# GpSimd's scatters in a graph kernel: a 128x112 product ahead of each, in place of one one-element operation per slot of 17

## What is computed

```python
xn = _layernorm(x)
x = x + L0_gnn(xn, src, dst)          # edge softmax: gathers x[src] for every edge, sums by dst
      + L0_mix(xn)                    # linear attention and an MLP, dense
x = x + L0_ffn(_layernorm(x))         # top-k of the nodes, MLP
xn = _layernorm(x)
x = x + L1_gnn(xn, edge_weight, W, b, src, dst) + L1_mix(xn)
x = x + L1_ffn(_layernorm(x))         # two chosen experts

def _L1_gnn_ref(x, edge_val, W, b, edge_row, edge_col):
    support = jnp.matmul(x, W)
    gathered = support[edge_col] * edge_val[:, None]
    out = jax.ops.segment_sum(gathered, edge_row, num_segments=x.shape[0])
    return out + b
```

## Time and profile before

| | us |
|---|---|
| median of three runs | 6699.03 |
| span of the profiled execution | 9414.7 |
| GpSimd busy in it | 4691.2 |
| of that, 1564 scatters (line 557) | 1532.7 |
| of that, 3128 gathers (line 1794) | 2980.2 |
| TensorE busy | 5293.0 |
| VectorE busy | 3692.5 |

### The profile page before, as it was taken

The page is one execution under the profiler, slowest core; times in us unless marked ns, Lnnn a source line. Parts: engine busy times, 40 slices in busy tenths (PEclk is TensorE's granted clock), DMA queues, the critical chain, the costliest instruction groups (busy, mean ns, idle before and its releaser), DMA issues. The chain is left out here.

```text
span 9414.7 us, 116831 instructions
## 1 busy us (share of the span) xinstructions
PE 5293.0 (56%) x22154; PEld 3875.0 (41%) x22155; DVE 3692.5 (39%) x14368; ACT 1980.3 (21%) x4706; POOL 4691.2 (50%) x5589
## 2 busy tenths in 40 slices
PE   0431176777777777786055371089444444444479
PEld 0320154555555555554044360078333333333367
DVE  6340154444444445555143240046333333333345
ACT  6110043333333333333011120023000000000034
POOL 3476501555555555554725427600566666666600
PEclk9775577888888888887577685599777777777789
DMA  2100000333333333332000000000233333333300
GB/s 78 28 4 3 5 1 22 89 86 85 83 84 80 78 81 82 78 80 78 3 1 3 2 19 5 5 7 1 70 91 90 91 91 91 90 91 90 91 27 18
DMA packets 505062, 495.27 MB, mean 53 GB/s; under 512 B 374733, under 2 KB 401878, under 8 KB 504150
## 3 DMA queue, kind: packets, MB, share of 16 engines
q0 software_dynamic: 200192, 432.72, 16.8%
q1 hardware_dynamic: 154712, 33.52, 2.0%
q10 hardware_dynamic: 150013, 27.32, 1.7%
HBM read 462.90 MB, written 30.23 MB: 52 GB/s over the span
## 5 line engine op out<-in xcount | busy, mean ns | idle before, releaser
L1794 POOL DMA_INDIRECT XN<-table,XN x3128 | 2980.2, 953 | 990.0 <-issue 934.5
L557 POOL DMA_INDIRECT records<-slot_rec,slot_pos x1564 | 1532.7, 980 | 598.5 <-issue 598.5
L2098 PE MATMUL gcn_psE<-XN,gcn_pE 128*125 x3520 | 1120.2, 482 | 1218.7 <-DVE gcn_pE L2114 911.1
L75 POOL TENSOR_TENSOR cell<-cell 1x1 int32<-1x1 int32 x874 | 164.1, 188 | 2674.5 <-DMA XN<-records 967.0
L2098 PEld LDWEIGHTS gcn_psE<-XN,gcn_pE 128*125 128x125 f32 x3520 | 823.5, 243 | 1515.3 <-issue 1354.9
L1923 PE MATMUL gat_psE<-XN,gat_pE 128*125 x3520 | 1046.0, 448 | 253.9 <-issue 173.3
L1923 PEld LDWEIGHTS gat_psE<-XN,gat_pE 128*125 128x125 f32 x3520 | 738.9, 221 | 397.1 <-issue 277.9
L2126 DVE TENSOR_TENSOR X<-X,gcn_psE 125x256 f32 x440 | 184.3, 419 | 1538.6 <-remote 1063.1
L1907 PE MATMUL gat_psS<-XN,gat_kTs 25*125 25x512 f32 x880 | 579.4, 742 | 181.3 <-ACT XN L1952 162.3
L2114 DVE TENSOR_SCALAR gcn_pE<-iota_n,gcn_lk,gcn_rec 128x125 f32<-128x125 f32 x1760 | 501.4, 363 | 16.0
L2180 ACT ACT_TABLE_LOAD x1 | 1.3, 1283 | 2345.4 <-PEq L117 2345.4
(11 more groups left out here) (453 smaller groups left out, 8451.4 us busy)
## 6 DMA issues: line engine op xcount, KB each, us to landing
XN<-table,XN POOLq DMA_INDIRECT x3128
records<-slot_rec,slot_pos POOLq DMA_INDIRECT x1564
XN<-records SPq DMA_DIRECT2D x782, 6.0 KB
gat_rec<-records ACTq DMA_DIRECT2D x440, 6.0 KB
gcn_rec<-records ACTq DMA_DIRECT2D x440, 6.0 KB
table<-XN ACTq DMA_DIRECT2D x5, 1250.0 KB
table<-room ACTq DMA_DIRECT2D x25, 250.0 KB
out_x<-X SPq DMA_DIRECT2D x25, 250.0 KB
```

Source lines behind the costliest of these rows:

```text
L557: pool.indirect_dma_start(out=rec_d[1], out_offset=bass.IndirectOffsetOnAxis(ap=slot_pos[:, h, j:j + 1], axis=0), in_=slot_rec[:, h, j, :] ...
L1794: pool.indirect_dma_start(out=rows_t[:, s, j, :], out_offset=None, in_=table, in_offset=bass.IndirectOffsetOnAxis(ap=rec_g[:, s, j, 1:2].b ...
L2098: last = pe.matmul(psE[d][0:B, 0:D], pE[:, d, j, :], rows_t[:, slot_of(g), j, :].rearrange("p a w -> p (a w)"), start=(j == 0), stop=(j == ...
```

## The change

In `Turns.pool` the settling addition ahead of a slot's scatters goes. Ahead of every scatter GpSimd now multiplies two reads of a 128x112 piece of the constant `ones` into a new tile `spacing`, having waited for the product before this one. Everything else, the loads, the scatters, their order and their number, stays. `Mover`, which moves records only where the edges come unsorted, and the edge walks keep their `settle`.

```diff
+SPACING = 112
@@
+        spacing = sb(ctx, "spacing", [P, SPACING])
@@ class Turns
-                self.settled = sem(name + "_settled")
+                self.spaced = sem(name + "_spaced")
@@ Turns.pool
                 with loop(pool, self.turns) as i:
                     for h in range(2):
                         pool.wait_ge(self.filled[h], i * 32 + 32)
-                        settle(pool, cell[0:1, 0:1], self.settled, i * 2 + h)
                         for j in range(SLOT):
+                            pool.wait_ge(self.spaced, i * (2 * SLOT) + h * SLOT + j)
+                            pool.tensor_tensor(spacing[:, :], ones[:, 0:SPACING], ones[:, 0:SPACING], ALU.mult).then_inc(self.spaced, 1)
                             pool.indirect_dma_start(
                                 out=rec_d[1], out_offset=bass.IndirectOffsetOnAxis(ap=slot_pos[:, h, j:j + 1], axis=0),
                                 in_=slot_rec[:, h, j, :], in_offset=None).then_inc(sent[h], 16)
```

## The result

The changed kernel takes 7210.57 us (median of 4 runs, 7209.37 to 7223.4), the kernel before 6698.62 (4 runs). The ratio is 1.0766, 95% interval 1.0752 to 1.0779. The forecast was slower by 322 us; the measured +512 lies inside the range of 6600 to 7280 us, near its upper end, and 190 us above the forecast.

A forecast was written before the change was run, and what follows sets the result against it. GpSimd's scatter queue was to become what ends both layers, once products outgrow the cover of other work: head 10 + first layer 168 + second layer 144 = +322 us on 6699, about 7020, range 6600 to 7280 us.

The forecast's parts named there:

- The head's +10 us: Head of the sort: no cover there, so its 34 scatters at 0.28 us more each add 10 us.
- I use 1.10: Timed runs: an indirect DMA is issued every 1.0 to 1.2 us, taken as 1.10, against 1.26 in the profile.
- the cover: Both layers: scatters before end at 928 under work to 960, and at 1079 under 1180; after, late by 168 and 144.
- took the stalls out: Profiled layers: 600 us of stall removed from the first, 1010 from the second, leaving 770 and 1180 us of work.
- +0.28: Outside the scans: each product widens the scatter pitch by 0.28 us, profile pitch 1.26 becoming 1.54, timed 1.10 becoming 1.38.
- The bound of some 7350: Upper end of the likeliest case: pitch 1.20 before and +0.42 per product give 14 + 282 + 359 us.
- The wait: Ahead of each product: it waits for the product one scatter earlier, done over 1 us before, so never blocks.
- Nothing is queued on SP, … only later: SP and ACT queues: the change adds nothing; SP's next-slot loads wait for the same counts, only later.
- The first, real stalls that the spacing ends: Scatter stretches: stalls S partly real in timed runs and ended by spacing; 6699 + 322 - S, 6420 for S = 600; chance 0.20.
- The second, no change: Scatters: something other than GpSimd's work sets a 1.3 to 1.4 us pitch, so products fill idle time; 6700 us; chance 0.13.
- Its other form, 150 us more work in each layer: Both layers: some 150 us more work in the runs than the stall-free figures gives the same 6700 us.
- the third, both sides holding each other up: Layers' scans: DVE's scans also slow by a quarter, 7020 + 95, about 7115 us; chance 0.10.

The follow-up runs named there:

- undisturbed profile: The kernel before, with no edit, profiled three more times: times 6702.21, 6699.97 and 6701.84 us, spans 6700.5, 6698.3 and 6700.2.
- experiment 5: 128x1 products ahead of each scatter without the wait, one settling operation per slot, against the kernel before: 6922.30 us, ratio 1.0331.
- width 1: The changed kernel with SPACING 1 instead of 112, so 128x1 products; compared with the kernel before: 6912.86 us, ratio 1.0317.
- width 56: The changed kernel with SPACING 56 instead of 112, so 128x56 products; compared with the kernel before: 7084.0 us, ratio 1.0571.
- experiment 4: The kernel before with only the first of each slot's 17 scatters issued, sorted tensor filled by one direct copy: 6510.22 us, ratio 0.9719.

## Why the prediction held, and which step was off

**The direction and the mechanism held.** GpSimd's queue ends both layers, each walk begins when the block has closed, and the product runs behind the scatter. One word of it was wrong: the queue did not become what ends the layers, it was that before. The head's +10 us were measured as +10.6 (last scatter 197.0 against 186.4).

**The step that failed: "I use 1.10", and the cover built on it.** The prediction saw rightly that the 9414.7 us could not be the timed kernel, and took the stalls out. But it then spread the missing time over the gathers and let scatters follow every 1.10 us in the timed runs. The pitch is 1.27 outside the scans in an undisturbed profile (0.96 + 0.30), the very figure of the first one. The kernel before has no cover. Its first layer's scatters end at 1014, not 928, after other work that ends at 969 (forecast 960). In the second layer they run without a pause from 3040 to 4251, 1211 us and not 1079, while the other work is done 1119 us after the first of them and not 1180. Of these 61 us too many, 54 lie in the top-k search: I took 235 us of stall out of it, but its last round begins 388 us after the layer's first scatter in the first profile and 100 in the second, 288 less.

The 190 us between forecast and measurement come out of this. Of them 133 are the cover that I took off, 32 in the first layer and 101 in the second. The other 57 are in the growth of the scatters' own chain: 10 + 200 + 245 = 455 in the forecast, 11 + 202 + 301 by the walks' starts (512 in the runs). In the second layer the forecast let the last 408 scatters of the kernel before wait for their places until 630 us, which the first profile suggested; undisturbed they never wait, so all 918 products count in full. That the first layer's chain grew by the forecast 200 us is luck, two errors against each other: products beside the scans were priced at +0.75 us each and cost half, the others at +0.28 and cost 0.32.

The bound of some 7350 has a slip too: with the pitches stated for the case of +0.28 beside the scans (2.2 and 1.65), a pitch of 1.62 elsewhere gives 291 and 313 us, not 282 and 359, some 7320 in all.

What should have told me: I took a part of GpSimd's gap of 0.30 us for disturbance, but it was equal to 0.01 us in undisturbed stretches, in the stalled ones' first 100 us and in both walks. And the walks' groups came to 5.25 us by the sum, 5.13 by the earlier trace rows; I explained this away by giving the first walk 5.65. In fact both walks run at 5.07 us a group (1980/391), GpSimd's own pace; PE's "busy" time of 2210 us in the first walk had shrunk to 1860 once the disturbance was gone.

**The price of a product.** +0.28 was forecast outside the scans, +0.32 measured. The product is shorter (0.38 for 0.415), but the scatter behind it grew from 0.96 to 1.01 us, and 0.04 us stand ahead of it. Beside the scans I expected 2.2 us from scatter to scatter. These are GpSimd's groups from 300 to 550 us, after:

```profile
L560 POOL DMA_INDIRECT records<-slot_rec,slot_pos x141 | 159.5, 1132 | 23.1 <-issue 23.1
L559 POOL TENSOR_TENSOR spacing<-ones 128x112 f32<-128x112 f32 x140 | 64.2, 458 | 4.0
```

and before:

```profile
L557 POOL DMA_INDIRECT records<-slot_rec,slot_pos x178 | 195.2, 1097 | 52.6 <-issue 52.3 <-DMA slot_pos<-spill_pos 0.3
L75 POOL TENSOR_TENSOR cell<-cell 1x1 int32<-1x1 int32 x11 | 3.1, 282 | 0.2
```

By the sum of busy and idle time over the count: 1.78 us after, 1.41 before, +0.37. The product takes 458 ns here and not 970. Three settling operations had given me a mean of 744 ns, and I added all their excess to the product; eleven in the undisturbed profile give 282.

**The wait** is free, as said (experiment 5).

**"Nothing is queued on SP, … only later" left out what the later loads hold up; it had no price.** In the second layer DVE now waits 136 us for a transfer (DVE's timeline of the changed kernel):

```profile
4060.15 0.17 DVE L1524 COPY b_nshift<-ones 125x2 f32<-125x2 f32 x1 [135.96 <-DMA spill_pos<-room]
```

In SP's queue the store it waits for stands behind the loads of the slots:

```profile
4056.86 0.33 SPq L542 DMA_DIRECT2D slot_rec<-spill_rec  x1
...
4058.03 0.35 SPq L1123 DMA_DIRECT2D spill_pos<-room  x1
```

SP issues the store of the last places only after the loads of the turns ahead of it, and each of these waits for scatters. Slower scatters so hold up the store, the store holds up DVE's release of the rows, and the last dense loop starts at 4067, some 135 us later than it could. The same wait is 55 us at width 1 and 103 at width 56, and neither the kernel before nor the one with products in the first layer alone has it. The layer's other work still ends at 4531, long before the last scatter at 4768, so the wait costs nothing here; with fewer scatters behind it it could, which no run tests.

**The rivals.** The first, real stalls that the spacing ends, is out: the kernel before has none in three undisturbed profiles, and 1.37 us (width 1) behaves like 1.59. The second, no change, is out: GpSimd has no idle time to fill but the 0.30 us gap, 0.16 of which stays behind the product. Its other form, 150 us more work in each layer, is out by experiment 4: without the scatters the layers end earlier, not at the same time. Of the third, both sides holding each other up, the traces show a little: DVE's 128x408 scans take longer (groups on DVE from 397 to 480 us, after):

```profile
L221 DVE TENSOR_TENSOR_SCAN room<-room,base 128x408 f32<-128x408 bf16 x36 | 39.0, 1121 | 0.0
```

and from 383 to 463 us, before:

```profile
L219 DVE TENSOR_TENSOR_SCAN room<-room,base 128x408 f32<-128x408 bf16 x37 | 37.4, 1048 | 0.0
```

1121 ns against 1048, 7%. It goes with the products' width: at width 1 the mean over the first layer is 1052. All of the layer's scans together take 114 us instead of 104. The layer's other work ends at 993 instead of 969, but 11 us of that are the head's, and the three profiles of the kernel before differ by 14 among themselves (954 to 969), so what DVE lost is some 10 us. It adds nothing to the time, since the scatters end at 1227.

## What to carry to other kernels

Compare a profile's span with the timed runs before taking anything from it, and where they differ by 40%, take another profile or use only what agrees in every stretch: here the scatter's 0.96 us did, and its gap of 0.30 wherever the other engines ran. With 1.26 us and no cover my own +0.28 would have given 1564 x 0.28 = 438 us; the measured 0.32 gives 1530 x 0.32 + 11 = 500. When an engine's queue may be what ends a block, compare its last instruction with the others' last: 61 and 109 us of idle DVE before the walks, in the undisturbed profile, meant that each 0.33 us put into that queue 1564 times would be paid in full. Price an added operation by the start-to-start time over both neighbours, since it can lengthen the one behind it.

## What the runs showed that I had not expected

- One-element operations between indirect DMAs aren't nearly free on GpSimd: 1564 of 128x1 cost 211 us, 0.135 us each, for 0.20 us of execution.
- A wait against a register's value ahead of each costs nothing measurable (6922 us without it, but with 92 settling operations more; 6913 with it).
- The product costs 1.7 ns a column outside the scans, (0.385 - 0.20)/111.
- An execution of an unchanged kernel was recorded with a span of 9414.7 us, where three later ones had 6698 to 6701, with TensorE, VectorE and ScalarE nearly stopped beside the scatters. GpSimd's scatters took 0.96 us as ever, their gap 0.30 or 0.44. What caused it is open.
- GpSimd's issue of indirect DMAs bounds nearly the whole kernel: before, from the first to the last scatter or gather, 45 us in the head, 814 and 1211 in the layers and 1981 and 1986 in the walks, 6037 of 6700 us. I conclude that neither moving turns between the layers nor more dense overlap would shorten it, as the scatters hang over in both; no run tests that. None of the versions here beats the kernel before but the one that leaves scatters out.
